# Two conv blocks on one core: images cut in halves on partition groups, 3x3 convolutions as nine taps on 32x32 array tiles

## The chip, the cores and the metric

The kernel runs on one core of a Trainium2 chip. The metric is device time in microseconds, the median of several runs. All data is fp32, apart from one small bf16 mask constant.

## The reference, cut to what matters

Input x is (8, 32, 32, 32): 8 images, 32 channels, 32 rows, 32 columns. Two blocks follow each other.

```python
# block L0
xn = ln_last(x, ln1_g, ln1_b)                  # over the 32 columns of a row
q, k, v = [conv3x3(conv1x1(xn, w1), w3) for q, k, v]   # no bias: folded into one 3x3 each
score = einsum('bhpd,bhpe->bhde', k, q) / scale # 8 heads, d = 4 neighbouring columns
attn = einsum('bhpd,bhde->bhpe', v, softmax(score))
x = conv1x1(attn, o_w) + x
xn = ln_last(x, ln2_g, ln2_b)
gate, info = gelu(conv3x3(conv1x1(xn, g1), g3)), conv3x3(conv1x1(xn, i1), i3)   # 64 channels each
x = conv1x1(gate * info, r1) + x
# block L1
out = leaky_relu(instance_norm(conv3x3(x, conv1_w) + b), 0.2)
out1 = conv3x3(out, conv2_w) + b
mask = sigmoid(conv3x3(out, mask_w) + b)
xm = out * mask
q, k, v = conv1x1(xm), conv1x1(pad(xm)), conv1x1(pad(xm))
attn = softmax over the 3x3 neighbours of sum_c q * k
return x + out1 * mask + (1 - mask) * sum over neighbours attn * v
```

## The kernel before, in words

The images are worked on in four pairs. A partition is (row block r, channel c) with four blocks of 8 rows, so every partition holds 8 rows of both images: 128 partitions by 512 values.

A 3x3 convolution multiplies on TensorE (PE) with K = 3 x 32 partitions: before it, the tensor is copied into a "planes" buffer (`sh_ln2`, `sh_x2`, `sh_in`) that holds the whole image three times, shifted by one column from one group of 32 partitions to the next. `shift_copies` (L278) does it with copies of 32 partitions by about 512 values, spread over VectorE (DVE, L283) and ScalarE (ACT, L483). The shift in y is an offset in the plane, so three matmuls of K = 96 or 128 accumulate one output. LN1's result goes to `sh_ln1` in a like way, by columns modulo 4 (`slot_copies`, L295), with four groups: two of its copies are DMAs of SyncE (SP, L333), the others are on DVE (L298) and ACT.

The matmuls: `qk` (L1160, 128x128), `v_by_head`, `conv1`, `mask_conv` and `conv2` (L1149, L1260, M = 32, four outputs on four column tiles of the array), `gate_info` (L1217, K = 96, M = 128, 512 columns), `reduce_1`. The window attention works on units of 4x8 pixels with 6x10 keys: `window_q`, `window_k`, `window_scores`, `window_v`, `probs_transposed`, `window_out`. Weights of the 1x1 and 3x3 convolutions of block L0 are multiplied together once at the start on PE and copied by `folded_qkv` and `other_constants` on DVE. An instance norm's scale is multiplied into the weights by GpSimd (POOL); POOL also takes the powers -1/2 of the norms (L392) and the residual arithmetic.

The order on every engine is written out by hand, in `step(pair)` of each engine's block: while pair n is in block L1, pair n+1 is in the second half of L0 and pair n+2 in its first half. A loop runs the first of these steps, the second is written behind it, and then the last two pairs' back halves follow in an order of their own. Engines meet by counting semaphores only; each engine waits in program order, so what stands behind a waiting instruction waits as well.

Of the kernel before, what the change touches and what calls it, by code (L numbers as in the profile page):

```python
# [68 lines left out]

def build(nc, x, shape_consts, vectors, w1_qkv, w3_qkv, w1_gi, w3_gi, conv_w, l1_qkv, r1_t, out):
    with ExitStack() as ctx:
        def sb(name, shape, dt=F32):
            return ctx.enter_context(nc.sbuf_tensor(name, shape, dt))  # L100
# [1387 lines left out]
```

## Time and profile before

| | us |
|---|---|
| median of 3 runs | 258.87 (258.56 to 259.05) |
| the profiled execution | 257.9 |
| its span, first to last instruction | 256.4 |
| DVE busy | 192.4 (75%) |
| PE busy (matmul) | 182.8 (71%) |
| ACT busy | 129.3 (50%) |
| POOL busy | 76.1 (30%) |
| mean granted TensorE clock | 0.90 of full speed |

The page gives one profiled execution. Busy times are of one engine; engines overlap. The chain of waits is followed back from the last instruction, at each step to what released it. "issue" is time in which an engine waited for nothing that the profile shows. A source matmul in fp32 appears as two MATMULs, each with its weight load (LDWEIGHTS, row PEld); matmuls on different tiles of the array overlap, so a group's busy time is less than count times mean.

### The profile page before, as it was taken

The page shows a single profiled execution, that of the slowest core. Times are in us where ns is not written, and L with a number is a line of the kernel's source. Part 1 is how long each engine was busy: PE and PEld are TensorE (multiplying, and loading weights), DVE is VectorE, ACT ScalarE, POOL GpSimd, SP SyncE. Part 2 cuts the span into 40 slices and gives each one's busy share as a digit, 9 for nine tenths or more (in the row PEclk, how much of TensorE's full clock was granted, in tenths as well). Part 3 has the DMA queues.
Part 4 walks back from the last instruction along what each step waited for, and adds up shares of the span by engine and source line. Part 5 has one row for each costly group of instructions (what it writes and reads, how often), then busy time and mean ns, then how long its engine had stood idle before and what let it go on. Part 6 is the DMA issues. An engine that isn't in the chain of part 4 may idle for free.

```text
span 256.4 us, 4585 instructions
## 1 busy us (share of the span) xinstructions
PE 182.8 (71%) x1738; PEld 111.0 (43%) x1738; DVE 192.4 (75%) x426; ACT 129.3 (50%) x256; POOL 76.1 (30%) x56
## 2 busy tenths in 40 slices
PE   0508749897568957966998589976179977297763
PEld 0308529343146536434584448442034534146632
DVE  5498694883998999996979956549999348883552
ACT  2043161641675845566745563267545467514750
POOL 4754804031008026400182231000917100302341
PEclk9999997999889999995899957999659999867995
DMA  6311021000030000000002000000010000000101
GB/s 196 75 25 36 4 61 41 0 3 0 1 102 3 1 0 3 0 23 0 3 0 84 1 1 3 0 0 3 0 41 4 0 0 4 0 0 3 45 0 43
DMA packets 5190, 5.17 MB, mean 20 GB/s; under 512 B 3184, under 2 KB 3408, under 8 KB 5168
## 3 DMA queue, kind: packets, MB, share of 16 engines
q1 hardware_dynamic: 4928, 4.29, 5.9%
q10 hardware_dynamic: 240, 0.58, 0.8%
q8 instruction: 14, 0.23, 0.4%
q14 instruction: 8, 0.07, 0.1%
HBM read 3.30 MB, written 1.05 MB: 17 GB/s over the span
## 4 chain that ended last, share of the span: by engine, by line
DVE 43%; PE 36%; ACT 8%; issue 7%; DMA 3%; POOL 1%; SPq 1%; ACTq 0%; DVEq 0%
PE ps L1224 12%; DVE sh_in L283 6%; PE ps L1171 5%; PE ps L1260 5%; DVE sh_ln L298 3%; DVE sh_ln L283 3%; DMA w3b<-in_w_gi 3%; ACT sh_x L483 2%; PE ps L1151 2%; DVE ln_out L764 2%; PE ps L1232 2%; DVE sh_x L283 2%; PE ps L1316 2%; PE ps L1300 2%; DVE gi L866 2%
## 5 line engine op out<-in xcount | busy, mean ns | idle before, releaser
L392 POOL TENSOR_TENSOR ln_s<-ln_s,neg_half 128x16 f32<-128x16 f32 x8 | 23.4, 2924 | 98.5 <-DVE ln_s L747 98.5
L1224 PE MATMUL ps<-sh_ln,w_gi 96*128 96x512 f32 x96 | 42.4, 596 | 0.5 <-DVE sm L822 0.5
L483 ACT ACTIVATE sh_ln<-ln_out 32x512 f32<-32x512 f32 (+1 forms) x44 | 27.4, 622 | 22.0 <-DVE ln_out L772 15.3
L1171 PE MATMUL ps<-w_qk,sh_ln 128*128 128x128 f32 x192 | 26.6, 302 | 12.8 <-ACT sh_ln L483 12.8
L1260 PE MATMUL ps<-sh_in,w_in 128*32 128x256 f32 x384 | 26.2, 432 | 11.4 <-DVE sh_in L283 11.4
L1171 PEld LDWEIGHTS ps<-w_qk,sh_ln 128*128 128x128 f32 x192 | 25.4, 216 | 16.4 <-issue 16.4
L1224 PEld LDWEIGHTS ps<-sh_ln,w_gi 96*128 96x128 f32 x96 | 17.9, 190 | 22.1 <-issue 21.9
L1260 PEld LDWEIGHTS ps<-sh_in,w_in 128*32 128x32 f32 x384 | 13.0, 124 | 23.3 <-DVE sh_in L283 12.5
L866 DVE TENSOR_TENSOR gi<-ps,gate 64x512 f32<-64x512 f32 x16 | 11.1, 694 | 15.0 <-ACT gate L518 14.7
L518 ACT ACTIVATE gate<-ps 64x512 f32<-64x512 f32 x16 | 9.3, 587 | 20.2 <-PE ps L1224 20.2
L283 DVE COPY sh_in<-act_c 32x496 f32<-32x496 f32 (+1 forms) x28 | 17.2, 614 | 0.5
L1151 PE MATMUL ps<-sh_x,w_conv 128*32 128x512 f32 x96 | 12.7, 664 | 5.7 <-DVE sh_x L283 4.4
L483 ACT ACTIVATE sh_x<-x 32x496 f32<-32x496 f32 (+1 forms) x20 | 12.3, 616 | 5.1 <-DVE x L873 4.9
L483 ACT ACTIVATE sh_in<-act_c 32x496 f32<-32x496 f32 (+1 forms) x20 | 12.3, 616 | 4.8 <-DVE act_c L931 4.5
L298 DVE COPY sh_ln<-ln_out 32x512 f32<-32x512 f32 x32 | 13.4, 418 | 0.5
L416 POOL TENSOR_TENSOR omm<-ones,msk 128x512 f32<-128x512 f32 x4 | 6.6, 1648 | 22.7 <-DVE msk L949 22.6
L499 ACT ACTIVATE qk_t<-ps 128x512 f32<-128x512 f32 x8 | 4.8, 596 | 15.5 <-PE ps L1171 15.5
L283 DVE COPY sh_x<-x 32x496 f32<-32x496 f32 (+1 forms) x28 | 11.5, 411 | 0.5
L283 DVE COPY sh_ln<-ln_out 32x496 f32<-32x496 f32 (+1 forms) x28 | 11.5, 411 | 0.5
L1181 PE MATMUL ps<-sh_ln,w_v 128*32 128x512 f32 x96 | 11.1, 596 | 0.0
L1316 PE MATMUL ps<-k_h,q_bd 128*64 128x60 f32 x256 | 10.8, 246 | 0.0
L398 POOL TENSOR_TENSOR inorm_v<-inorm_v,neg_half 128x2 f32<-128x2 f32 x4 | 4.3, 1076 | 21.9 <-DVE inorm_v L924 21.9
(129 smaller groups left out, 358.5 us busy)
## 6 DMA issues: line engine op xcount, KB each, us to landing
x_norm<-in_x SPq DMA_DIRECT2D x4, 256.0 KB, 2.7
x_res<-in_x SPq DMA_DIRECT2D x4, 256.0 KB, 2.5
out_x<-out_s SPq DMA_DIRECT2D x4, 256.0 KB, 2.0
sh_ln<-ln_out SPq DMA_DIRECT2D x8, 64.0 KB, 2.1
kc<-in_shape_consts ACTq DMA_DIRECT2D x1, 450.0 KB, 6.6
w3b<-in_w_gi SPq DMA_DIRECT2D x1, 288.0 KB, 6.5
vec<-in_vectors SPq DMA_DIRECT2D x1, 131.5 KB, 3.3
w3a<-in_w_qkv ACTq DMA_DIRECT2D x1, 108.0 KB, 3.2
```

The lines of the kernel that those rows point to most:

```text
L283: ins = copy(plane(planes)[C * s:C * s + C, :, 1 + RH * r:1 + RH * r + RH, cut_left:cut_left + n], src[C * r:C * r + C, :, :].rearrange("p ...
L298: ins = copy(slot_planes(s, r), slots_of(s, r))
L392: nc.gpsimd.tensor_tensor(ln_s[n][:, 3, :], ln_s[n][:, 2, :], neg_half[:, :], ALU.pow)\
L483: return nc.scalar.activation(o, i, ACT.Copy)
L518: nc.scalar.activation(gate[EC:P, n, :], ps[0:EC, GI_BANKS[n], :], ACT.Gelu).then_inc(g_gelu.sem, 1)
L866: nc.vector.tensor_tensor(gi[EC * (n % 2):EC * (n % 2) + EC, n // 2, :], ps[EC:P, GI_BANKS[n], :], gate[EC:P, n, :], ALU.mult).then_inc(g_ ...
L1151: mm = nc.tensor.matmul(ps[C * r:C * r + C, bank, :], weight(dy), plane(planes)[:, :, RH * r + dy:RH * r + dy + RH, 0:W], start=(dy == 0), ...
L1171: mm = nc.tensor.matmul(to, sh_ln1[:, d, i, WD * y:WD * y + P], w_qk[:, dy, :, :, :].rearrange("p d m c -> p (d m c)"), start=(dy == 0), s ...
L1181: mm = nc.tensor.matmul(ps[C * d:C * d + C, 2, :], w_v[:, dy, :], sh_ln1[:, d, :, WD * dy:WD * dy + WD * H], start=(dy == 0), stop=(dy == 2))
L1224: mm = nc.tensor.matmul(ps[:, GI_BANKS[2 * i + h], :], w_gi[:, dy, :, :].rearrange("p m o -> p (m o)"), xs[:, i, y:y + H // 2, 0:W], start ...
L1260: mm = nc.tensor.matmul(ps[C * r:C * r + C, bank, BLK * i:BLK * i + BLK], w_in[:, i, k, dy, :], plane(sh_in)[:, i, RH * r + dy:RH * r + dy ...
L1316: mm = nc.tensor.matmul(ps[C * r:C * r + 2 * C, 5 + bank, KEYS * n:KEYS * n + KEYS], q_bd[:, u, r:r + 2, :].rearrange("p r m -> p (r m)"), ...
```

## The change

- A partition is now (image i, half h, channel c): group g = 2i + h of 32 partitions holds 16 rows of one image. `ln2_out`, `x2` and `xm` are stored with a border of one pixel, (16 + 2) x 34; the row across the cut between the halves is copied by `edge_copies`, four copies of 32 partitions by 34 values on ACT. `x_in` holds all four pairs, and most buffers exist twice, by pair modulo 2.
- A 3x3 convolution is nine matmuls with K = 32, one for each tap, read straight from the bordered tile with offsets in y and x: `gate_info` on the four row tiles of the array (M = 128), `conv1` and the refine convolutions (mask and conv2) on all 16 tiles of 32x32, with weights repeated on the four partition groups. Their outputs are strips: four strips of 4 rows (`STRIP` = 128 values) for each group, in four banks. `conv1` turns the layout from (group, strip) to (strip, group); the refine convolutions turn it back, with an identity matmul for the activation itself.
- The planes of `sh_x2`, `sh_in` and `sh_ln2` and their copies are gone. Those of LN1 stay: for pair 0 by DVE, ACT and 4 DMAs, for the other pairs by 16 DMAs of 64 KB each from SP.
- The instance norm is applied by ACT as scale and bias when it reads conv1's result from PSUM (POOL multiplies mean and rstd for the bias); the weights are no longer scaled. `act_s` has its rows above and below copied by ACT (`rows_above`) and DVE (`rows_below`).
- `window_scores` uses 32x32 tiles, `window_out` K = 60 and M = 32 with 32 columns, `attn_out` M = 32. q is no longer spread out in a block-diagonal buffer; `key_windows` is 4 ACT instructions a pair, not 16.
- POOL's clears of the large planes shrink to borders. x is loaded by four DMAs a pair, the result stored by four.
- There is no loop; each engine's program is one list over all four pairs, in a new order. The front halves of all pairs are finished earlier, and the back halves of pairs 2 and 3 run interleaved at the end, with PSUM banks 4 to 7 for pairs 0 to 2 and 0 to 3 for pair 3.

The core of the diff (indentation cut by 12):

```diff
+HALF = HH * W
+STRIP = HALF // R
+SH = HH // R
...
-def shift_copies(copy, src, planes, s, row_blocks):
-cut_left, cut_right = max(1 - s, 0), max(s - 1, 0)
-n = W - cut_left - cut_right
-for r in row_blocks:
-    ins = copy(plane(planes)[C * s:C * s + C, :, 1 + RH * r:1 + RH * r + RH, cut_left:cut_left + n],
-               src[C * r:C * r + C, :, :].rearrange("p i (y x) -> p i y x", x=W)
-               [:, :, :, cut_right:cut_right + n])
-return ins
-def slot_copies(copy, s, row_blocks):
-for r in row_blocks:
-    ins = copy(slot_planes(s, r), slots_of(s, r))
-return ins
+def edge_copies(copy, t):
+for g in (0, 2):
+    copy(t[rows32(g), HH + 1, :], t[rows32(g + 1), 1, :])
+    ins = copy(t[rows32(g + 1), 0, :], t[rows32(g), HH, :])
+return ins
...
-        sp.dma_start(slot_planes(1, r), slots_of(1, r)).then_inc(planes_by["ln1"]["dma"].sem, 16)
+def ln1_planes(pair):
+    wait_done(sp, g_ln[0], pair)
+    wait_done(sp, g_v4, pair - 2)
+    for g in range(R):
+        for s in range(R):
+            sp.dma_start(half_planes(pair, s, g), half_slots(pair, s, g)).then_inc(s_ln1[pair], 16)
...
+load(0, (0, 1))
+sp.dma_start(vec[:, :], vectors).then_inc(s_vec, 16)
+load(1, range(R))
+sp.dma_start(w1b[:, :], w1_gi).then_inc(s_wb, 16)
+sp.dma_start(w3b[:, :, :, :], w3_gi).then_inc(s_wb, 16)
+sp.wait_ge(s_pad, 4)
+wait_done(sp, g_ln[0], 0)
+for g in range(R):
+    sp.dma_start(half_planes(0, 1, g), half_slots(0, 1, g)).then_inc(s_planes["dma"], 16)
+load(2, range(R))
+sp.wait_ge(s_zero_bd, Z_BD)
+for r in range(R):
+    sp.dma_start(w_bd[rows32(r), :, rows32(r)], l1_qkv).then_inc(s_diag, 16)
+for h in range(2):
+    sp.dma_start(w_r1[EC * h:EC * h + EC, h, :], r1_t).then_inc(s_diag, 16)
+ln1_planes(1)
+for r in range(R):
+    for dx in range(3):
+        sp.dma_start(w_conv[rows32(r), dx, :, :, :], conv_w[C * dx:C * dx + C]).then_inc(s_diag, 16)
+load(3, range(R))
+ln1_planes(2)
+ln1_planes(3)
...
+def ln2_edges(pair):
+    wait_done(act, g_ln[1], pair)
+    edge_copies(copy, ln2_out).then_inc(g_edge2.sem, 1)
+def rows_above(pair):
+    t = act_s[pair % 2]
+    wait_done(act, g_lr, pair)
+    for j in range(1, R):
+        copy(t[rows32(j), 0, :, :], t[rows32(j - 1), SH, :, :])
+    copy(t[rows32(0), 0, 1:R:2, :], t[rows32(R - 1), SH, 0:R:2, :]).then_inc(g_up.sem, 1)
...
+def other_constants():
+    dve.wait_ge(s_fold, 2)
+    for s in range(3):
+        gi_f = ps[:, 4 + s, 0:6 * EC].rearrange("p (m y o) -> p m y o", m=2, o=EC)
+        nc.vector.tensor_copy(w_gi[:, :, s, :, :].rearrange("p y m o -> p m y o"), gi_f)\
+          .then_inc(s_wready, 1)
...
+def rows_below(pair):
+    t = act_s[pair % 2]
+    wait_done(dve, g_lr, pair)
+    for j in range(R - 1):
+        nc.vector.tensor_copy(t[rows32(j), SH + 1, :, :], t[rows32(j + 1), 1, :, :])
+    nc.vector.tensor_copy(t[rows32(R - 1), SH + 1, 0:R:2, :], t[rows32(0), 1, 1:R:2, :]).then_inc(g_down.sem, 1)
...
+folded_qkv()
+ln1_center(1)
+ln_var(0, 1)
+other_constants()
+ln1_apply(1)
+dve.wait_ge(s_wready, W_ALL)
+heads(0)
+ln1_center(2)
+ln2_center(0)
+ln_var(0, 2)
+ln_var(1, 0)
+dve.wait_ge(s_zero, BORDERS + 1)
+ln1_apply(2)
+ln2_apply(0)
+heads(1)
+ln1_center(3)
+ln_var(0, 3)
+ln1_apply(3)
+gated(0)
+x2_sum(0)
...
+inorm(2)
+inorm_mean(2)
+variance(2)
+inorm(3)
+inorm_mean(3)
+variance(3)
+activation(2)
+activation(3)
+masked(2)
+masked(3)
...
+def fold_gate_info():
+    pe.wait_ge(s_wb, 32)
+    pe.wait_ge(s_zero_bd, Z_BD + 6)
+    for m in range(2):
+        for s in range(3):
+            for r in range(R):
+                mm = nc.tensor.matmul(ps[rows32(r), 4 + s, 3 * EC * m:3 * EC * m + 3 * EC],
+                                      w1b[:, C * m:C * m + C], w3b[:, s, m, :], start=True, stop=True)
+    mm.then_inc(s_fold, 1)
...
-    for h in range(2):
-        for dy in range(3):
-            y = H // 2 * h + dy
-            mm = nc.tensor.matmul(ps[:, GI_BANKS[2 * i + h], :],
-                                  w_gi[:, dy, :, :].rearrange("p m o -> p (m o)"),
-                                  xs[:, i, y:y + H // 2, 0:W], start=(dy == 0), stop=(dy == 2))
-        mm.then_inc(g_i.sem, 1)
+def gate_info(pair, dy):
+    if dy == 1:
+        wait_done(pe, g_ln[1], pair)
+    else:
+        wait_done(pe, g_edge2, pair)
+    for dx in range(3):
+        for g in range(R):
+            mm = nc.tensor.matmul(ps[:, g, :], w_gi[rows32(g), dy, dx, :, :].rearrange("p m o -> p (m o)"),
+                                  ln2_out[rows32(g), dy:dy + HH, dx:dx + W],
+                                  start=(dy == 1 and dx == 0), stop=(dy == 2 and dx == 2))
+            if dy == 2 and dx == 2:
+                mm.then_inc(g_i.sem, 1)
-    for dy in range(3):
-        for r in range(R):
-            mm = nc.tensor.matmul(ps[C * r:C * r + C, bank, :], weight(dy),
-                                  plane(planes)[:, :, RH * r + dy:RH * r + dy + RH, 0:W],
-                                  start=(dy == 0), stop=(dy == 2))
+    for dy in (1, 0, 2):
+        wait_done(pe, g_x2e, pair)
+        for dx in range(3):
+            for j in range(R):
+                for g in range(R):
+                    mm = nc.tensor.matmul(ps[rows32(j), b + g, S_CONV:S_CONV + STRIP],
+                                          w_conv[rows32(g), dx, 0, dy, :],
+                                          t[rows32(g), SH * j + dy:SH * j + dy + SH, dx:dx + W],
+                                          start=(dy == 1 and dx == 0), stop=(dy == 2 and dx == 2))
-    for i in range(2):
-        for dy in range(3):
-            for r in range(R):
-                mm = nc.tensor.matmul(ps[C * r:C * r + C, bank, BLK * i:BLK * i + BLK],
-                                      w_in[:, i, k, dy, :],
-                                      plane(sh_in)[:, i, RH * r + dy:RH * r + dy + RH, 0:W],
-                                      start=(dy == 0), stop=(dy == 2))
+    for dy in (1, 0, 2):
+        if dy == 0:
+            wait_done(pe, g_up, pair)
+        if dy == 2:
+            wait_done(pe, g_down, pair)
+        for dx in range(3):
+            for g in range(R):
+                for j in range(R):
+                    mm = nc.tensor.matmul(ps[rows32(g), b + j, col:col + STRIP],
+                                          w_conv[rows32(j), dx, k, dy, :],
+                                          t[rows32(j), dy:dy + SH, g, dx:dx + W],
+                                          start=(dy == 1 and dx == 0), stop=(dy == 2 and dx == 2))
...
+    for g in range(R):
+        for j in range(R):
+            nc.tensor.matmul(ps[rows32(g), b + j, S_ACT:S_ACT + STRIP],
+                             kc[rows32(j), K_ID + C * j:K_ID + C * j + C], t[rows32(j), 1:1 + SH, g, 1:1 + W],
+                             start=True, stop=True)
+    refine_conv(pair, 2, S_MASK)
+    refine_conv(pair, 1, S_CONV).then_inc(g_rf.sem, 1)
...
+pe.wait_ge(s_ln1[1], 256)
+for i in range(2):
+    qk_banks_read(1, i)
+    qk(1, i)
+attn_out(0)
+v_by_head(1)
+gram(1)
+by_head(1)
+pe.wait_ge(s_ln1[2], 256)
+for i in range(2):
+    qk_banks_read(2, i)
+    qk(2, i)
+pe.wait_ge(s_wready, W_ALL)
+pe.wait_ge(s_diag, 16 * (R + 2 + 3 * R))
+front_read(0, 1, 2)
+for dy in (1, 0, 2):
+    gate_info(0, dy)
+reduce_1(0)
...
```

On PE, after `reduce_1(0)`: attn_out(1), v_by_head(2), conv1(0), gram(2), average_mean(0), by_head(2), average_var(0), gate_info(1), refine(0), reduce_1(1), attn_out(2), qk(3, 0), window_q(0), window_k(0), qk(3, 1), window_scores(0), window_v(0), v_by_head(3), gram(3), by_head(3), probs_transposed(0), window_out(0), conv1(1), gate_info(2, 1), average_mean(1), gate_info(2, 0), average_var(1), gate_info(2, 2), refine(1), reduce_1(2), attn_out(3), the window steps of pair 1 with gate_info(3) between window_v(1) and probs_transposed(1), reduce_1(3), then conv1(2), its averages, conv1(3), its averages, refine(2), refine(3), q and k windows of 2 and 3, scores and v of 2, of 3, transposes and window_out of 2, of 3.

## Rows read from the trace of the kernel before

**Rows 1.** the page's busy row: us, share of the span, instructions

```profile
PE 182.8 (71%) x1738; PEld 111.0 (43%) x1738; DVE 192.4 (75%) x426; ACT 129.3 (50%) x256; POOL 76.1 (30%) x56
```

**Rows 2.** the page's chain of waits, share of the span by engine

```profile
DVE 43%; PE 36%; ACT 8%; issue 7%; DMA 3%; POOL 1%; SPq 1%; ACTq 0%; DVEq 0%
```

**Rows 3.** timeline of PE, the starts of conv1 (start us, us, what)

```profile
67.40 4.32 PE L1151 MATMUL ps<-sh_x,w_conv 128*32 128x512 f32 x24 [2.96 <-DVE sh_x L283]
...
123.62 2.78 PE L1151 MATMUL ps<-sh_x,w_conv 128*32 128x512 f32 x24 [0.34 <-DVE sh_x L283]
...
175.24 2.78 PE L1151 MATMUL ps<-sh_x,w_conv 128*32 128x512 f32 x24 [1.10 <-DVE sh_x L283]
```

**Rows 4.** windows: stretch, us, busy (instructions) by engine, clock, DMA share, GB/s

```profile
0.00:67.40 67.40, 40.00 (x246) 26.11 (x247) 48.58 (x109) 25.32 (x41) 25.02 (x18) 0.97 0.16 42
67.40:123.60 56.20, 44.35 (x424) 26.14 (x425) 51.27 (x115) 35.03 (x70) 14.07 (x9) 0.91 0.06 15
123.60:175.20 51.60, 44.41 (x424) 27.27 (x424) 37.75 (x86) 27.72 (x58) 13.71 (x10) 0.90 0.04 12
175.20:256.40 81.20, 54.02 (x644) 31.46 (x644) 54.79 (x119) 41.18 (x89) 23.30 (x19) 0.83 0.03 11
```

**Rows 5.** groups by line: count, busy us, mean ns, idle us before them

```profile
L1224 PE MATMUL ps<-sh_ln,w_gi 96*128 96x512 f32 x96 | 42.4, 596 | 0.5 <-DVE sm L822 0.5
L483 ACT ACTIVATE sh_ln<-ln_out 32x512 f32<-32x512 f32 (+1 forms) x44 | 27.4, 622 | 22.0 <-DVE ln_out L772 15.3 <-DVE ln_out L764 6.3
...
L283 DVE COPY sh_in<-act_c 32x496 f32<-32x496 f32 (+1 forms) x28 | 17.2, 614 | 0.5
L298 DVE COPY sh_ln<-ln_out 32x512 f32<-32x512 f32 x32 | 13.4, 418 | 0.5
...
L866 DVE TENSOR_TENSOR gi<-ps,gate 64x512 f32<-64x512 f32 x16 | 11.1, 694 | 15.0 <-ACT gate L518 14.7
...
L563 ACT ACTIVATE xw<-xm 128x60 f32<-128x60 f32 x64 | 9.6, 247 | 0.0
...
L518 ACT ACT_TABLE_LOAD x4 | 5.1, 1283 | 0.1
...
L513 ACT ACTIVATE sm<-sm 128x8 f32<-128x8 f32 x4 | 0.8, 208 | 4.3 <-DVE sm L824 4.3
```

**Rows 6.** chain of waits in order of time (start us, us, what)

```profile
41.13 2.91 POOL ln_s L392
...
240.43 0.67 DVE wsm L989
```

**Rows 7.** windows of window_out's matmuls alone, at two clocks

```profile
171.90:173.10 1.20, 1.10 (x64) 0.97 (x64) 1.00 0.00 0
250.00:252.00 2.00, 1.92 (x64) 1.72 (x64) 0.50 0.04 8
```

**Rows 8.** timeline of the SP queue's issues

```profile
0.73 0.39 SPq L312 DMA_DIRECT2D x_norm<-in_x  x1
...
3.53 2.57 SPq L322 DMA_DIRECT2D w_bd<-in_l_qkv  x4
...
16.47 1.35 SPq L333 DMA_DIRECT2D sh_ln<-ln_out  x2
```

**Rows 9.** DMA view: a queue's packets, MB, share; an issue's KB and landing

```profile
q8 instruction: 14, 0.23, 0.4%
...
sh_ln<-ln_out SPq DMA_DIRECT2D x8, 64.0 KB, 2.1
```

**Rows 10.** timeline of the start

```profile
4.55 0.69 DVE L734 TENSOR_REDUCE ln_s<-x_norm 128x16 f32<-128x512 f32 x1 [1.35 <-DMA vec<-in_vectors]
...
13.31 2.94 DVE L771 COPY ln_out<-ln_out 128x112 f32<-128x112 f32 x1
...
20.41 7.36 PE L1171 MATMUL ps<-w_qk,sh_ln 128*128 128x128 f32 x48 [8.33 <-ACT sh_ln L483]
...
27.82 0.50 DVE L771 COPY ln_out<-ln_out 128x112 f32<-128x112 f32 x1
```

More of the change, by code:

```diff
@@ L540, in q_evac @@
             def q_evac(pair):
-                act.wait_ge(g_q.sem, g_q.done(pair))
-                act.wait_ge(g_s.sem, g_s.before(pair))
-                for r in range(R // 2):
-                    rows = slice(C * r, C * r + C)
-                    nc.scalar.activation(q_bd[rows, :, r, :],
-                                         ps[rows, 4, :].rearrange("p (u m) -> p u m", u=UNITS), ACT.Identity,
-                                         bias=vec[rows, V_BQ:V_BQ + 1]).then_inc(g_q_sb.sem, 1)
@@ new lines, in _ @@
+            window_softmax(0)
+            ln2_apply(2)
+            v_evac(0)
+            window_probs(0)
+            heads(3)
+            inorm(1)
+            inorm_mean(1)
+            variance(1)
+            activation(1)
+            gated(2)
+            masked(1)
+            x2_sum(2)
+            ln2_center(3)
+            ln_var(1, 3)
+            window_softmax(1)
+            ln2_apply(3)
+            v_evac(1)
+            window_probs(1)
+            gated(3)
+            x2_sum(3)
@@ L1166, in qk @@
+                mm.then_inc(s_fold, 1)
+            def qk(pair, i):
+                for h in range(2):
                     for d in range(0, D, 2):
@@ new lines, in _ @@
+            by_head(3)
+            probs_transposed(0)
+            window_out(0)
+            back_banks_read(0)
+            conv1(1)
+            front_read(2, 3, 3)
+            gate_info(2, 1)
+            average_mean(1)
+            gate_info(2, 0)
+            average_var(1)
+            gate_info(2, 2)
+            refine(1)
+            reduce_1(2)
+            attn_out(3)
+            window_q(1)
+            window_k(1)
+            window_scores(1)
+            window_v(1)
+            front_read(3, 3, 3)
@@ new lines, in _ @@
+            for dy in (1, 0, 2):
+                gate_info(3, dy)
+            probs_transposed(1)
+            window_out(1)
+            reduce_1(3)
+            back_banks_read(1)
+            conv1(2)
+            average_mean(2)
+            average_var(2)
+            conv1(3)
+            average_mean(3)
+            average_var(3)
+            refine(2)
+            refine(3)
+            window_q(2)
+            window_k(2)
+            window_q(3)
+            window_k(3)
+            window_scores(2)
```

1467 lines of the change are left out of this document (633 added, 834 removed).

## The prediction

> **What bounds the kernel now.** The busy row [rows 1] has DVE at 192.4 of 256.4 us and PE at 182.8, neither full; the chain of waits [rows 2] gives DVE 43% and PE 36%. They hand work to each other in order, and the question is what that hand-over becomes. Cut at the starts of conv1 of pairs 0, 1 and 2 [rows 3], the windows [rows 4] are front A 67.4 us, stage B 56.2, stage C 51.6, tail D 81.2 (the back halves of two pairs). I price the new program in the same four pieces.
>
> **What it takes away and adds, by engine.** DVE and ACT made all shifted planes. On DVE that is 13.4 us for LN1's rows and 17.2 for act's [rows 5], with two more L283 groups of 11.5: 53.6; with the q_bd copies, centring and scaling some 65 of 192 us go. On ACT it is 27.4 and two groups of 12.3, some 50 of 129. In their place come edge copies of 32 partitions by 34 to 136 elements. No row has them on ACT; they lie between 208 ns for 8 elements and 247 for 60 (the larger ones below 627) [rows 5]; I take 0.22, and 0.30 for 136 elements. The added POOL product of two elements has no row; between nothing and the 2.9 us of the power [rows 6] I take 0.25, as it is a plain product.
>
> PE gets many more, smaller matmuls, because the shift in x moves from the plane's partitions into nine taps. A source matmul is two MATMULs in the trace (gate/info's 12 a pair: 96/4 = 24). MATMULs a pair: gate/info 24 to 72 (K 32, M 128, 512 columns), conv1 24 to 288, refine 96 to 608 (K 32, M 32, 128 columns), scores 64 to 128, window_out 64 to 128. The price hangs on how many row tiles run side by side, and the trace has only column tiles. Its rows: a full-array pass of 512 columns is 42.4/96 = 0.44 us [rows 5]; 64 MATMULs of 64 columns on four column tiles take 1.10 us at clock 1.0 and 1.92 at 0.5 [rows 7]. By the first, 64 columns on a quarter of the array stream in 0.44/8/4 = 14 ns, so the 1.10 is streaming (0.9) and one drain, and to issue a MATMUL with its weight load costs 14 ns or less. Bounds: 16 tiles side by side stream 128 columns in 0.11 us, 6.9 ns a MATMUL: conv1 2.0 us, refine 4.2, gate/info 9 x 2 x 0.44 = 7.9; no overlap of row tiles, 27.5 ns: conv1 7.9, refine 16.7, gate/info 31.7. I take 8.3 ns, near the first, because column tiles come that near to their limit: conv1 2.4, refine 5.0, gate/info 7.9 (10.6 before).
>
> [...]
>
> **Front A.** Here a wait is added. LN1's planes of pairs 1 to 3 were two DMAs and copies; now they are 16 DMAs a pair from the one SP queue. Two took 1.35 us to issue and four 2.57: 0.64 each [rows 8], and one lands 2.1 after its issue [rows 9]. So 15 x 0.64 + 2.1 = 11.7 us lie between LN1's end and qk. Behind that wait PE holds attn_out and v_by_head, for them waits LN2 of the pair before, and behind that on DVE LN1 of the next pair. The steps:
> - vec is issued behind two quarters of x, 0.75 later: LN1(0) starts at 5.3 (before 4.55 [rows 10]). Three operations of 0.7, squares 0.6, variance: 3.0; POOL's power 2.95 [rows 6]; apply 1.9; slot copies 0.6 (2.94 under POOL's clears, 0.5 without [rows 10], and the clears are gone): 13.8.
> - First planes by eight DVE copies 3.5, folded weights 0.9: qk(0) at 18.2 (before 20.4). It takes 7.4 as now [rows 10], v_by_head 2.8, the folding of the gate weights, now behind them, 1.9: 30.4. DVE waits for it in other_constants: 2.6, then apply LN1(1) 2.4: 35.4. The scores of pair 0 hide behind the next wait.
> - planes(1) 11.7: 47.1. qk(1) 7.2 (PE starts cold again), attn_out 1.1: 55.4.
> - x1 and centre 2.9, variance 0.9, power 2.95, apply LN1(2) 2.4: 64.6. planes(2) 11.7: 76.3. qk(2) 7: 83.3.
> - ACT's exp of heads(1) stands behind the evacuation of qk(2): 0.8; head_mix 2.3, then on DVE LN1(3), 2.1 + 0.9 + 2.95 + 2.4, ahead of gated(0): 94.8. gate/info(0) hides beside that. gated 4 x 0.7 [rows 5], reduce 1.1: 98.7; attn_out(1) and v_by_head(2) 3.9: conv1(0) at 102.6.
> So A costs 35 us more, 23 of them the two DMA waits.
>
> **Stages B to D**, walked the same way: an operation of 512 columns is 0.6 to 0.7 us on DVE and ACT [rows 5], a small one 0.2, a hand-over 0.05, POOL's power 3.0 (1.1 on two elements), a table load 1.3 [rows 5].
> B, from conv1(0)'s start: conv1, statistics, averages and heads(2), LN2(1) interleaved, to the variance 9.7; power and product 1.5, inorm_apply 0.9, leaky relu and rows above 2.0; only then does ACT copy LN2's edges (0.9), for which gate/info(1) waits 2.8 with dy 0 and 2: edges 15.0, gate 20.3, refine 25.3. tanh, out1, mask 2.2: 27.5. PE meanwhile runs reduce, attn_out, qk(3,0), q and k windows to 32.8, qk(3,1) 2.7, scores 2.6: 38.1. On DVE softmax, LN2(2), v_evac to 42.4, probabilities 3.1, the start of heads(3) 0.9; by_head, transposes, evacuation 2.1: 48.5; window_out 1.3, its evacuation 1.0: 50.9.
> C: conv1, two thirds of gate/info and the averages 8.3; variance to leaky relu 3.4; refine 5.1: 16.8; table, tanh, out1, mask 3.2: 20.0; q and k windows and evacuations 5.2; scores(1) 1.4, softmax 2.7, LN2(3) 1.4: 30.7; gate/info(3) 7.9: 38.6; transposes, window_out, evacuation 4.0; table and gelus, gates, reduce 5.8: 48.4.
> D: conv1 and statistics of pair 2, then of 3 (activation(2) stands behind variance(3)) 11.5; leaky relu and rows 2.0; two refines, the first in part beside the rows, to 22.6; tanh to mask of pair 3 and the q, k evacuations to 27.7; scores(2), v(2), scores(3), v(3) on PE 9.0, DVE ending softmax(3) at 38.7; v_evac and probabilities 4.3, transposes and evacuation 1.2, window_out 1.4, final 1.6, four stores 4.3: 51.5. Before, 16 us lie between the last maximum and the end [rows 6]; here 15.4.
>
> Sum: 102.6 + 50.9 + 48.4 + 51.5 = 253.4, all of B to D at full clock. Now D has clock 0.83 with PE busy 54 of 81 us [rows 4]; the new program has more gaps ahead of dense bursts (refine(2), the last transposes, reduce(3), conv1(2)), and a burst at 0.5 takes nearly twice as long [rows 7]: I add 6, between 0 and 12. 259.4; the profiled execution is 1.5 above its span (257.9 and 256.4): 260.9; the median of the runs is 1.0 above that execution: **262 us**.
>
> **Rivals.**
> (1) The front is cheaper than walked. If DMAs follow each other at 0.35 us (x_norm's issue alone took 0.39 [rows 8]) and the stages overlap a little better, A ends at 91 and B to D give 147: 238, with the 2.5 of above **240**. For it: the tail alone gives back 30 us, and DVE falls to some 125. Against: 0.64 is much the same in each burst of the trace. It decides from A below 99. 0.36.
> (2) PE is slower on small tiles. 5500 MATMULs for 1738 need some 0.7 MB of instructions against 0.23 in 14 packets, each 0.4% x 16 x 256 / 14 = 1.2 us long [rows 9]. A refine uses 4.7 packets in 5 us. If they come one per 2.5 us, a MATMUL costs 20 ns: conv1 5.6, refine 12, so 10 us in B, 10 in C, 20 in D: **300**. Half of that, 280, where row tiles overlap only in part. 0.20. Against: no MATMUL of the trace waits there, but none comes so fast.
> (3) Not a rival in sign: tiles at 7 ns and a warm PE, 253. Within the forecast's own range.
> The forecast, 250 to 274, holds 0.44. The range that leaves out a tenth at either end is 236 to 292. Less than 0.2%, 0.5 us, can't be told from no change: 0.04. Faster 0.39 (case 1 and the lower end of the forecast), slower 0.57.
>
> **What would show it.** Right: PE idle some 10 us before qk(1) and qk(2), released by a DMA; conv1(0) starting near 102; DVE busy near 125; D near 55. Wrong: planes landing less than 8 us after LN1's end; a refine above 7 us at clock 1.0; PE gaps with "issue" as releaser inside a refine.

## The result, and the profile after

| | before | after |
|---|---|---|
| median | 258.96 us (258.56 to 259.19, 4 runs) | 324.51 us (320.67 to 326.11, 4 runs) |
| profiled execution, its span | 257.9, 256.4 | 320.67, 318.9 |
| its mean granted TensorE clock, 1.00 at full speed | 0.900 | 0.853 |
| ratio | | 1.2433, 95% interval 1.2347 to 1.2519 |

The changed kernel is a quarter slower. The forecast was 262 us, and its range ended at 292. Here and below a ratio compares only the fast runs of two kernels (some executions are slower at a lower granted clock, as 326.11 us at 0.835 beside 320.67 at 0.853), so it isn't the quotient of the two medians.

First the page of the kernel after: the busy row, the instruction queue and the chain's shares; then three groups of PE (count, busy us, mean ns, idle us before them and what ended it). "PEld" is PE's weight loads.

```profile
PE 198.0 (62%) x5630; PEld 142.3 (45%) x5630; DVE 123.8 (39%) x295; ACT 82.4 (26%) x186; POOL 52.7 (17%) x60
...
q8 instruction: 44, 0.72, 1.0%
...
PE 50%; DVE 18%; issue 13%; SPq 6%; POOL 5%; ACT 4%; DMA 2%; POOLq 0%; DVEq 0%; ACTq 0%
...
L1116 PE MATMUL ps<-act_s,w_conv 32*32 32x128 f32 x2304 | 37.8, 298 | 23.0 <-issue 23.0
...
L1063 PE MATMUL ps<-ln_out,w_gi 32*128 32x512 f32 x288 | 35.9, 642 | 5.6 <-DVE ln_out L753 4.5
...
L1089 PE MATMUL ps<-x,w_conv 32*32 32x128 f32 x1152 | 20.3, 321 | 7.3 <-issue 6.3
```

DVE lost 68.6 us of its work against [rows 1], and ACT 46.9, as intended. PE has 15 us more, and the chain's "issue" share went from 7% [rows 2] to 13% of a longer span, 41 us. The two small-tile convolutions (refine L1116, conv1 L1089) have 29.3 us of idle time that ends with "issue": PE waited for nothing that a semaphore or a DMA of the kernel explains.

The windows of the kernel after, cut at the same events as [rows 4], the starts of conv1 of pairs 0, 1 and 2:

```profile
0.00:104.74 104.74, 51.86 (x426) 37.23 (x427) 45.72 (x107) 17.38 (x34) 17.18 (x31) 0.80 0.22 55
104.74:169.76 65.02, 48.26 (x1402) 34.29 (x1399) 28.84 (x75) 22.79 (x53) 10.34 (x7) 0.90 0.03 7
169.76:234.80 65.04, 45.08 (x1386) 27.89 (x1386) 23.97 (x48) 21.98 (x47) 12.79 (x10) 0.92 0.04 11
234.80:318.90 84.10, 52.79 (x2424) 42.94 (x2420) 25.32 (x66) 20.20 (x52) 12.40 (x12) 0.82 0.04 10
```

| stage | before | forecast | after | off by |
|---|---|---|---|---|
| A, front | 67.4 | 102.6 | 104.7 | 2.1 |
| B | 56.2 | 50.9 | 65.0 | 14.1 |
| C | 51.6 | 48.4 | 65.0 | 16.6 |
| D, tail | 81.2 | 51.5 | 84.1 | 32.6 |

A is as walked. The error lies in B, C and D, which hold one, one and two refine convolutions. The PE timeline of pair 0's refine in the kernel after shows what one looks like (start us, us, what, count, idle before and its end):

```profile
127.84 2.24 PE L1116 MATMUL ps<-act_s,w_conv 32*32 32x128 f32 x149
131.36 1.92 PE L1116 MATMUL ps<-act_s,w_conv 32*32 32x128 f32 x128 [1.28 <-issue]
134.81 1.92 PE L1116 MATMUL ps<-act_s,w_conv 32*32 32x128 f32 x128 [1.53 <-issue]
138.26 1.92 PE L1116 MATMUL ps<-act_s,w_conv 32*32 32x128 f32 x128 [1.53 <-issue]
141.72 0.89 PE L1116 MATMUL ps<-act_s,w_conv 32*32 32x128 f32 x42 [1.54 <-issue]
```

PE runs exactly 128 MATMULs in 1.92 us, stands still, and starts the next 128 just 3.45 us after the last start. With their weight loads these are 256 instructions. From the identity matmuls at 127.40 to the end, refine takes 15.2 us. The DMA view of 127 to 143 us of the same kernel has nothing in it but the instruction queue (the first line is GB/s in 40 slices of 0.4 us, a packet standing in the slice in which it starts):

```profile
GB/s 0 0 0 0 0 41 0 0 0 0 0 0 0 41 0 0 0 0 0 0 0 0 41 0 0 0 0 0 0 0 41 0 0 0 0 0 0 0 0 0
...
q8 instruction: 4, 0.07, 1.5%
```

Four packets of some 16 KB, at about 129.0, 132.5, 135.9 and 139.3, one to a burst and never two together: each starts about 1.1 us after a burst does, takes 1.0 us (1.5% of 16 engines over 16 us, by four), and the next burst starts some 1.4 us behind its end. That makes the step of 3.45.

### The profile page after: what moved, and what is told of

Read it like the earlier page. It is cut to its first block, busy times and chain, and to the rows that moved or that the text cites. A ratio compares the mean times of both kernels' runs of the same rounds, so it can differ in the third digit from the quotient of the medians.

```text
span 318.9 us, 12069 instructions
## 1 busy us (share of the span) xinstructions
PE 198.0 (62%) x5630; PEld 142.3 (45%) x5630; DVE 123.8 (39%) x295; ACT 82.4 (26%) x186; POOL 52.7 (17%) x60
## 3 DMA queue, kind: packets, MB, share of 16 engines
HBM read 2.59 MB, written 1.05 MB: 11 GB/s over the span
## 4 chain that ended last, share of the span: by engine, by line
PE 50%; DVE 18%; issue 13%; SPq 6%; POOL 5%; ACT 4%; DMA 2%; POOLq 0%; DVEq 0%; ACTq 0%
PE ps L1116 12%; PE ps L1004 9%; PE ps L1063 8%; PE ps L1089 6%; SPq L241 6%; POOL ln_s L286 3%; PE ps L1161 2%; DVE gi L760 2%; DVE ln_d L651 2%; PE ps L1017 2%; PE ps L1072 2%; DVE ln_out L674 1%; PE ps L1197 1%; DMA sh_ln<-ln_out 1%; PE ps L1138 1%
## 5 line engine op out<-in xcount | busy, mean ns | idle before, releaser
L1116 PE MATMUL ps<-act_s,w_conv 32*32 32x128 f32 x2304 | 37.8, 298 | 23.0 <-issue 23.0
L1116 PEld LDWEIGHTS ps<-act_s,w_conv 32*32 32x32 f32 x2304 | 30.7, 107 | 29.4 <-issue 27.3
L1004 PEld LDWEIGHTS ps<-w_qk,sh_ln 128*128 128x128 f32 x192 | 29.3, 245 | 30.1 <-DMA sh_ln<-ln_out 19.0
L1063 PE MATMUL ps<-ln_out,w_gi 32*128 32x512 f32 x288 | 35.9, 642 | 5.6 <-DVE ln_out L753 4.5
L1063 PEld LDWEIGHTS ps<-ln_out,w_gi 32*128 32x128 f32 x288 | 16.2, 199 | 21.1 <-issue 19.9
L1089 PE MATMUL ps<-x,w_conv 32*32 32x128 f32 x1152 | 20.3, 321 | 7.3 <-issue 6.3
L1089 PEld LDWEIGHTS ps<-x,w_conv 32*32 32x32 f32 x1152 | 16.1, 113 | 13.0 <-issue 11.8
L1072 PE MATMUL ps<-gi,w_r 128*32 128x512 f32 x32 | 6.0, 833 | 11.2 <-DVE gi L760 11.2
L418 ACT ACTIVATE hn<-ps,inorm_v 128x256 f32<-128x256 f32 x8 | 4.1, 566 | 24.7 <-POOL inorm_v L295 24.6
L1034 PEld LDWEIGHTS ps<-sc_d,kc 128*128 128x128 f32 x8 | 1.8, 280 | 18.4 <-DVE sc_d L701 14.1
L366 ACT ACTIVATE p_t<-ps 128x512 f32<-128x512 f32 x8 | 4.6, 596 | 20.9 <-PE ps L1182 20.9
```

Of the source, the lines that this page charges most:

```text
L366: return nc.scalar.activation(o, i, ACT.Copy)
L1004: mm = nc.tensor.matmul(to, sh_ln1[pair % 2][:, d, i, WD * y:WD * y + P], w_qk[:, dy, :, :, :].rearrange("p d m c -> p (d m c)"), start=(d ...
L1063: mm = nc.tensor.matmul(ps[:, g, :], w_gi[rows32(g), dy, dx, :, :].rearrange("p m o -> p (m o)"), ln2_out[rows32(g), dy:dy + HH, dx:dx + W ...
L1072: mm = nc.tensor.matmul(ps[rows32(g), 1, :], w_r1[:, g % 2, :], gi[:, g // 2, :], start=True, stop=True)
L1089: mm = nc.tensor.matmul(ps[rows32(j), b + g, S_CONV:S_CONV + STRIP], w_conv[rows32(g), dx, 0, dy, :], t[rows32(g), SH * j + dy:SH * j + dy ...
L1116: mm = nc.tensor.matmul(ps[rows32(g), b + j, col:col + STRIP], w_conv[rows32(j), dx, k, dy, :], t[rows32(j), dy:dy + SH, g, dx:dx + W], st ...
```

## Experiments

S names the theory that PE starves for instructions: a packet of 128 MATMULs with their weight loads every 3.45 us, whatever they are. Of the rivals, T says that the small tiles are slow of themselves, and W that something else holds PE up; their forms are spelled out in the expectations. Where a kernel ran once, its one time is given, to be held against the profiled execution of the kernel after, 320.67. That was the fastest of its four, which go up to 326.11, so a few us of a single run prove nothing. "..." in an edit marks what is left out.

**One row of taps.** The conv1 and refine loops of the changed kernel run over one row of taps, so two thirds of the taps are missing from the result.

```diff
...
-for dy in (1, 0, 2):
+for dy in (1,):
     for dx in range(3):
...
```

> The kernel after, with only the middle tap row (dy = 1) of conv1 and of the two refine convolutions; two thirds of these taps are left out of the result. MATMULs a pair: conv1 96 for 288, refine 224 for 608. Theory S (PE's instructions arrive in packets of 128 MATMULs, one per 3.45 us): a refine falls from 15.2 us to about 5.5, conv1 from 6.1 to about 2.5, and the span from 319 to 262 to 270, since nothing else changes and the chain runs through them. Theory T (the 32x32 tiles themselves are slow, 27 ns a MATMUL): the same fall, but with no issue gaps of 1.5 us after each 128 MATMULs. Theory W (my walk of the rest was wrong, and other waits hold B to D): the span stays above 285.

Measured: 263.22 us. Its windows, cut as above:

```profile
0.00:104.63 104.63, 51.54 (x426) 36.07 (x426) 46.16 (x107) 17.38 (x34) 17.18 (x31) 0.80 0.22 56
104.63:155.38 50.75, 39.25 (x826) 27.02 (x823) 28.29 (x74) 22.80 (x53) 10.34 (x7) 0.85 0.03 6
155.38:208.62 53.24, 38.82 (x810) 21.34 (x810) 24.08 (x48) 21.98 (x47) 12.79 (x10) 0.85 0.05 12
208.62:261.30 52.68, 34.55 (x1272) 27.24 (x1268) 25.07 (x66) 20.17 (x52) 12.41 (x12) 0.73 0.05 14
```

2304 MATMULs fewer give back 57.4 us, 25 ns each, three times the 8.3 ns of the forecast. A is untouched, so nearly all of what was wrong lies in these two convolutions. The instruction queue has 26 packets for 44: 18 fewer, and 2304 / 128 is 18. D falls to 52.7 though its granted clock is 0.73 for 0.82, so the half clock isn't what made D long.

**The kernel before, refine cut small.** No row tiles, no K of 32: the old column-tile matmuls, each cut from 256 columns to 64, four times as many.

```diff
-for dy in range(3):
-    for r in range(R):
+for y in range(0, RH, 2):
+    for dy in range(3):
+        for r in range(R):
...
```

> The kernel before, with each of the 96-MATMUL refine convolutions (mask and conv2 of a pair) cut into four times as many matmuls of 64 columns in place of 256: 384 MATMULs a pair, same weights, same column tiles, no row tiles, same streaming. Theory S: the two convolutions of a pair take about 10 us in place of 5.6, with gaps released by issue after each 128 MATMULs, and the time rises from 259 to 272 to 280. Theory T: column tiles are not slow (64 MATMULs in 1.10 us), so 384 take about 5.5 to 6 us and the time stays within 259 to 262.

Measured: 257.45 us, against 260.42 of the kernel before beside it, which in other runs took 253.6 to 260.4: no change that can be told. S's forecast, 272 to 280, failed. But the gaps are there, in the PE timeline of this kernel:

```profile
92.05 2.00 PE L1262 MATMUL ps<-sh_in,w_in 128*32 128x64 f32 x128 [1.28 <-issue]
95.78 0.52 PE L1262 MATMUL ps<-sh_in,w_in 128*32 128x64 f32 x18 [1.73 <-issue]
```

Again a burst of 128 MATMULs between stops of 1.3 and 1.7 us, and a step of 3.7. Packets rise from 14 [rows 9] to 23, 9 for 1152 more MATMULs. So the stops belong neither to row tiles nor to tiles of 32x32. The time didn't follow: only 5.5 us of such gaps in four pairs, since the first 150 to 285 MATMULs of a stretch come from the supply in hand and 384 a pair leave little behind them. The mechanism is shown here, not its price.

**Two queues for LN1's planes.** Half of the 16 transfers a pair issue from ACT's queue.

```diff
...
-for s in range(R):
+for s in range(2):
     sp.dma_start(half_planes(pair, s, g), half_slots(pair, s, g)).then_inc(s_ln1[pair], 16)
...
+for s in range(2, R):
+    act.dma_start(half_planes(pair, s, g), half_slots(pair, s, g)).then_inc(s_ln1[pair], 16)
...
```

> The kernel after, with the 16 DMAs of LN1's planes of a pair issued half from SP and half from ACT. If issue at 0.6 us each sets the wait before qk(1) and qk(2), both waits shrink by 8 issues, 5 us, and conv1(0) starts near 95 in place of 104.7, the time falls by 8 to 10 us to about 311 to 314. If the transfers themselves set it, nothing moves in A and the time stays at 320 to 326.

Measured: 308.19 us, below the 311 to 314 expected. The SP queue of the kernel after:

```profile
34.99 10.34 SPq L241 DMA_DIRECT2D sh_ln<-ln_out  x16
```

and both queues of this one, and its qk(1):

```profile
34.45 5.22 SPq L241 DMA_DIRECT2D sh_ln<-ln_out  x8
34.45 5.53 ACTq L507 DMA_DIRECT2D sh_ln<-ln_out  x8
...
42.16 7.55 PE L1014 MATMUL ps<-w_qk,sh_ln 128*128 128x128 f32 x48 [6.45 <-DMA sh_ln<-ln_out]
```

Issue was the price, 0.65 us a transfer on one queue, and halves on two. The waits ahead of qk(1) and qk(2) fall from 10.40 and 8.37 us to 6.45 and 3.98, and conv1(0) starts at 95.63, 9.1 us earlier. The other 3.4 us came in the stages behind: 1.6 less in B and 2.1 less in D, where the mean granted clock is 0.92 for 0.90 and 0.85 for 0.82, and 0.3 more in C; that is within what the runs of one kernel differ by.

**Column tiles in the inner loop.** Shown is conv1's loop; the refine loop is swapped the same way.

```diff
...
-for j in range(R):
-    for g in range(R):
+for g in range(R):
+    for j in range(R):
...
```

> The kernel after, with the two inner loops of conv1 and of the refine convolutions swapped: consecutive matmuls now go to different column tiles of one row tile (and one bank), not to different row tiles. Theory S (packets of 128 MATMULs, one per 3.45 us whatever their speed): within a burst the 13 ns a MATMUL may change either way, but the step from burst to burst stays 3.45 to 3.75 us and the time stays at 318 to 326. Theory T (the array's pace decides): the time moves by 10 us or more with the burst's pace.

Measured: 327.55 us, 1.5 above S's range, with a mean granted clock of 0.764 for 0.853. Pair 0's refine in this kernel:

```profile
129.60 1.92 PE L1116 MATMUL ps<-act_s,w_conv 32*32 32x128 f32 x128 [1.25 <-issue]
133.33 2.33 PE L1116 MATMUL ps<-act_s,w_conv 32*32 32x128 f32 x128 [1.81 <-issue]
136.78 2.81 PE L1116 MATMUL ps<-act_s,w_conv 32*32 32x128 f32 x128 [1.12 <-issue]
140.51 1.34 PE L1116 MATMUL ps<-act_s,w_conv 32*32 32x128 f32 x42 [0.91 <-issue]
```

The order of the tiles changes neither the burst (1.92 us, 15 ns a MATMUL and not the 13 of the expectation) nor the step. Then the granted clock fell from 1.00 to 0.50, and the bursts grew to 2.33 and 2.81 us; the steps stayed at 3.73, 3.45 and 3.73, and the stops shrank. The slower array did not lengthen them while the supply was the limit. The 6.9 us above 320.67 come with the lower clock (PE is busy 216.8 us for 198.0); whether the order had a part in that clock is open.

**Refine in bf16.** The activation and the weights of the refine stage are rounded to bf16: one MATMUL for each source matmul in place of two, 304 a pair for 608, the identity's among them.

```diff
-act_s = two("act_s", [P, SH + 2, R, PW])
+act_s = [sb(f"act_s_{n}", [P, SH + 2, R, PW], BF16) for n in range(2)]
+w_ref = sb("w_ref", [P, 3, 3, 3, C], BF16)
...
```

> [...] Theory S: a refine still needs 304 x 27 = 8.2 us with gaps after each 128 MATMULs, and the time falls by 4 x 7 = 28 us to about 292 to 297. [...]

Measured: 286.34 us. Pair 0's refine in this kernel, and the end of pair 3's, where two stand one behind the other:

```profile
126.49 1.64 PE L1120 MATMUL ps<-act_s,w_ref 32*32 32x128 bf16 x165
130.49 1.42 PE L1120 MATMUL ps<-act_s,w_ref 32*32 32x128 bf16 x123 [2.35 <-issue]
...
246.11 1.47 PE L1120 MATMUL ps<-act_s,w_ref 32*32 32x128 bf16 x128 [1.77 <-issue]
249.57 1.47 PE L1120 MATMUL ps<-act_s,w_ref 32*32 32x128 bf16 x128 [1.98 <-issue]
253.30 0.32 PE L1120 MATMUL ps<-act_s,w_ref 32*32 32x128 bf16 x9 [2.26 <-issue]
```

The burst of 128 is shorter (1.47 us at a granted clock of 0.50, for 1.92 at 1.00 in fp32), the stop longer by as much, and the steps are 3.46 and 3.73 as in fp32: the type doesn't enter the supply. Refine(0) takes 5.5 us, less than the expectation's S had for it and less than half of 15.2, because the first 165 of its 288 come from the supply in hand; a total 6 us below what S gave fits that. 34.3 us for 1216 MATMULs are 28 ns each, near the 25 of the row of taps.

**Refine's taps in a hardware loop.** The same number of MATMULs run; 5 taps of 9 are written out. The waits for the rows above and below (`g_up`, `g_down`) now stand ahead of all taps.

```diff
...
+tap(1, 0, start=True)
+with pe.Fori(0, 3):
+    tap(1, 1)
+    tap(1, 2)
+tap(2, 1)
+return tap(2, 2, stop=True)
```

> The changed kernel with the same count of MATMULs executed in each refine convolution, but their taps in a hardware loop: one tap written out, a loop of three passes over a body of two taps (64 MATMULs), two taps written out. The taps repeat, so the result of the convolution isn't the reference's. S (PE starves for its instruction packets, which bring 128 MATMULs each 3.45 us): the body is fetched once if a branch back finds it in the buffer, so 5 taps of 9 are fetched, refine falls from 15.2 us to 9 to 11 and the time to 290 to 302. W (the gaps come from running 128 small MATMULs in a row, whatever fetched them): refine stays near 15 us, time 316 to 326. S with a branch that throws the buffered instructions away: gaps of 2 us or more at each of the six branches back, refine 17 us or more, time above 322.

Measured: 300.30 us. Pair 0's refine in this kernel, and the end of pair 3's; then its windows:

```profile
127.76 8.83 PE L1114 MATMUL ps<-act_s,w_conv 32*32 32x128 f32 x575
...
263.91 3.46 PE L1114 MATMUL ps<-act_s,w_conv 32*32 32x128 f32 x214 [1.78 <-issue]
```

```profile
0.00:105.47 105.47, 51.69 (x427) 36.21 (x427) 46.17 (x107) 17.38 (x34) 17.19 (x31) 0.81 0.23 56
105.47:163.46 57.99, 46.91 (x1403) 33.25 (x1400) 28.40 (x74) 22.80 (x53) 10.35 (x7) 0.93 0.02 6
163.46:224.65 61.19, 48.17 (x1386) 29.80 (x1386) 23.48 (x48) 21.98 (x47) 12.54 (x10) 0.86 0.04 11
224.65:298.50 73.85, 51.79 (x2424) 41.06 (x2420) 25.37 (x66) 20.18 (x52) 12.45 (x12) 0.85 0.04 11
```

This settles it. In pair 0 the same tiles, columns, banks and count run through without a stop, 14.8 us becoming 8.8, and over the four pairs one stop of 1.8 us is left where there were 23.0 us of them; the kernel is 20.4 us faster, while PE's busy time over the whole of it is the same (198.6 for 198.0 us). The packets fall to 36: 8 fewer, and the 4 taps that a loop repeats are 128 MATMULs of each of 8 convolutions, 1024 / 128 = 8. The branches of the loops cost nothing that the timeline shows. It also gives the array's own price: 15.4 ns a MATMUL. W and the variant in which a branch throws the buffered instructions away are out, and so is T: its 27 ns a MATMUL lies at the prediction's bound for row tiles that don't overlap at all (27.5), but that is chance, since the same tiles take 15.4 once they are fed. The repeated taps give a wrong convolution; a loop over the nine real taps, with offsets from registers, was not tried.

**Both edits at once**, two queues and the loop.

> The changed kernel with both edits at once: LN1's plane transfers half from ScalarE's queue, and the taps of the refine convolutions in a loop over a body of two taps (taps repeat, the result isn't the reference's). If the transfers' issue and the supply of instructions are two separate costs, their gains add: 320.7 less 12.5 less 20.4 (each from the profiled execution with one edit alone), 286 to 290. If they share a cause (the instruction packets wait behind the 64 KB transfers, or the other way round), the sum falls short: 294 or more.

Measured: 291.59 us, between the two expectations. The window up to conv1(0) in this kernel, and on the PE timeline the conv1 starts behind it:

```profile
0.00:96.34 96.34, 51.62 (x427) 36.13 (x427) 46.16 (x107) 17.38 (x34) 17.19 (x31) 0.82 0.25 63
```

```profile
154.52 4.22 PE L1099 MATMUL ps<-x,w_conv 32*32 32x128 f32 x173 [0.97 <-ACT pv L497]
...
215.88 3.31 PE L1099 MATMUL ps<-x,w_conv 32*32 32x128 f32 x185
```

A is 9.1 us below that of the loop alone, the same 9.1 as with two queues alone; B, C and D are 58.2, 61.4 and 73.9 us, where the loop alone has 58.0, 61.2 and 73.9. Stage by stage the two costs add. What doesn't repeat is the 3.4 us behind the front that the expectation had counted to the two queues.

**The tap gate alone, in the kernel before.** Only the gate and info convolution reads a bordered LN2 tile on row tiles; LN2's planes go. One thing more was changed, which the expectation doesn't say: in the tail, ACT's q and k evacuations and `key_windows` of pair 2 stand ahead of pair 3's gelus, and DVE's q evacuation ahead of its gate products. That order was not run by itself.

```diff
-w_gi = sb("w_gi", [3 * C, 3, 2, EC])
+w_gi = sb("w_gi", [P, 3, 3, 2, EC])
-ln2_out = sb("ln2_out", [P, 2, BLK])
+ln2_out = sb("ln2_out", [P, 2, RH + 2, PW])
...
-planes("ln2", ln2_out, sh_ln2, g_ln[1], g_i, pair)
+for r in range(R - 1):
+    act_copy(ln2_out[C * r + C:C * r + 2 * C, :, 0, :], ln2_out[C * r:C * r + C, :, RH, :])
+    ins = act_copy(ln2_out[C * r:C * r + C, :, RH + 1, :], ln2_out[C * r + C:C * r + 2 * C, :, 1, :])
...
```

> The kernel before with one part of the change alone: gate/info as nine taps on the four row tiles, read from a bordered LN2 tile in the old layout (8 rows of both images a partition), halo rows by 6 ACT copies; no planes of LN2, all else as before. MATMULs a pair 72 for 24, 512 columns each, 8 us in all, which is far above 27 ns each. Theory S: no issue gaps in this stage, it takes 8.0 us for 10.6, and with 12 plane copies a pair gone the time falls by 6 to 14 us, to 245 to 253. Theory T (row tiles are slow of themselves): gate/info above 10.6 us and the time not below 259.

Measured: 256.14 us (4 runs) against 258.89, ratio 0.9886 [0.9789, 0.9982]. No issue gap in the gate convolution: 288 MATMULs of 512 columns are few and long, and the instruction queue has 15 packets, one more than before. But I had expected 6 to 14 us and got 3. The ACT and PE timelines of this kernel show where the gain of the loop's pass went:

```profile
111.86 1.07 ACT L517 ACTIVATE gate<-ps 64x512 f32<-64x512 f32 x2 [5.54 <-PE ps L1238]
112.95 3.82 ACT L482 ACTIVATE sh_ln<-ln_out 32x512 f32<-32x512 f32 x6
116.68 1.05 ACT L517 ACTIVATE gate<-ps 64x512 f32<-64x512 f32 x2
...
118.75 1.93 PE L1247 MATMUL ps<-gi,w_r 128*32 128x512 f32 x8 [5.88 <-DVE gi L876]
```

The four banks now finish together, at the end of the ninth tap, so the gelus can't start while the convolution runs, and two of them stand behind LN1's slot copies, as they did before.

**Gelus ahead of ACT's slot copies.**

```diff
-if norm:
-    ln1_planes(pair + 3)
 gelu(pair + 1, 2)
 gelu(pair + 1, 3)
+if norm:
+    ln1_planes(pair + 3)
```

> The kernel before with its gate and info convolution alone on row tiles of the bordered tile, and in the one pass of ScalarE's loop the LN1 slot copies (3.82 us) put behind the last two gate gelus and not ahead of them. S and W (both theories of the refine convolutions) say the same here, since no small MATMULs were added: no issue gaps, and reduce_1 of that pass follows the gate convolution by about 3.5 us and not 7, so 250 to 255 us, 3 below the same kernel without the exchange (256.1). Against it: the slot copies are then 2 us later, and if q and k of the next pair wait for them, nothing is gained.

Measured: 255.61 us (12 runs), ratio to the kernel before 0.9955 [0.9887, 1.0023], above the expected range and not told from no change, and reduce_1 waits longer, 6.68 us for 5.88. The DVE timeline of this kernel names what was next:

```profile
113.37 3.44 DVE L297 COPY sh_ln<-ln_out 32x512 f32<-32x512 f32 x8
...
116.84 2.87 DVE L876 TENSOR_TENSOR gi<-ps,gate 64x512 f32<-64x512 f32 x4
```

All gelus are done at 114.11, and the products wait for DVE's own slot copies.

**Gate products ahead of DVE's slot copies too.**

```diff
-ln1_apply(pair + 3)
+ln_apply(0, ln1_out, "ln1", pair + 3)
+ln1_neighbours(pair + 3)
 gated(pair + 1, 0)
...
 gated(pair + 1, 3)
+if norm:
+    planes("ln1", ln1_out, sh_ln1, g_ln[0], g_v4, pair + 3)
```

> The kernel before with the tap gate and with the four gelus ahead of ScalarE's slot copies, and now the four gate products ahead of VectorE's slot copies of LN1 too (once in the kernel, in the loop's one pass). In the version without the last step the gelus ended at 114.11 and the products began at 116.84, behind 3.44 us of copies. If those copies are what is late, the products end near 116.4, reduce_1 comes 2.5 to 3 us earlier, and the time is 251 to 254. If the copies, now 3 us later, are what the next pair's q and k wait for (they start at 128.4), nothing is gained: 255 to 256.

Measured: 254.47 us (251.31 to 256.39, 12 runs) against 257.79 (253.99 to 259.68, 17 runs) of the kernel before on the same chip, ratio 0.9916 [0.9862, 0.9970]. The wait ahead of reduce_1 in this kernel, and the one behind it:

```profile
112.53 1.20 PE L1250 MATMUL ps<-gi,w_r 128*32 128x512 f32 x8 [2.54 <-DVE gi L876]
117.48 1.93 PE L1358 MATMUL ps<-p_t,v_t 128*32 128x64 f32 x64 [3.75 <-ACT p_t L579]
```

The first fell from 6.68 to 2.54 us, but window_out's matmuls now wait 3.75 us for ACT's copies of p_t, which stand behind ACT's slot copies. From the gate convolution's start to conv1's, the pass takes 20.4 us here, 21.7 in the version before and 20.9 with the tap gate alone. This version has the lowest median of the study, 0.8% below the kernel before by its ratio, and it keeps that kernel's loop and its other matmuls. What is shown is that the tap gate, with its order in the tail, makes the kernel before about 1% faster; the tap gate's own ratio is 0.9886, so nothing shows that the two exchanges on top of it add anything.

## Why the prediction was wrong

**Right.** The reading of the front. From PE's timeline of the kernel after:

```profile
46.86 7.51 PE L1004 MATMUL ps<-w_qk,sh_ln 128*128 128x128 f32 x48 [10.40 <-DMA sh_ln<-ln_out]
...
76.22 8.16 PE L1004 MATMUL ps<-w_qk,sh_ln 128*128 128x128 f32 x48 [8.37 <-DMA sh_ln<-ln_out]
85.22 8.01 PE L1063 MATMUL ps<-ln_out,w_gi 32*128 32x512 f32 x72 [0.84 <-issue]
...
104.74 2.59 PE L1089 MATMUL ps<-x,w_conv 32*32 32x128 f32 x174
109.11 1.78 PE L1089 MATMUL ps<-x,w_conv 32*32 32x128 f32 x114 [1.78 <-issue]
```

A takes 104.7 us for 102.6; qk(0), qk(1), qk(2) start at 17.34, 46.86 and 76.22 for 18.2, 47.1 and 76.3, the latter two behind idle times of 10.40 and 8.37 us that a DMA ends, and the 0.64 us an issue of [rows 8] held over sixteen in a row (0.65). Two queues show that this is issue. gate/info takes 8.01 us at a granted clock of 1.00 for 7.9, so four row tiles do overlap fully at 512 columns. DVE's busy time is 123.8 for about 125. Of "PE starts cold again" the traces show a slow start: the 48 MATMULs of qk(1) take 7.51 us for 7.2, and of them 19 fill the first 4.0 us, at a mean granted clock of 0.50; in qk(0) 18 fill the first 4.0 us, at 1.00. DVE's copy of `ln_out`, 2.94 us in [rows 10] beside POOL's clears, takes 0.22 in the kernel after, at 12.50 us, with no large clear beside it; the 0.50 of [rows 10] still had one. The front costs 37 us more than before, and that alone eats the 30 us that the tail was to give back.

**The step that failed** is the price of a small MATMUL, "I take 8.3 ns". conv1 took 6.15 us for 2.4 and refine 15.2 for 5.0. Two things were mis-sized in it:

- What the array does, when nothing starves it: 15.4 ns at a granted clock of 1.00, from the looped refine, not 8.3. I took the bound by streaming (6.9) as nearly reached because 64 MATMULs on four column tiles came near theirs [rows 7]. But by that row a MATMUL with its weight load needed no more than 14 ns, and that was an upper bound for issue that I read as a cost already hidden; the 15.4 lies just above it. In bf16 it is 9.9 (165 in 1.64 us at the same clock), so the 14 is no floor either. At a granted clock of 0.50 the bursts of 128 take 22.0 ns a MATMUL in fp32 (2.81 us) and 11.5 in bf16 (1.47 us). What sets 15.4 and 9.9 is not settled; the order of tiles isn't it (128 took 1.92 us in either order). The "one drain" in the 1.10 us was an estimate of mine, what is left beside 0.9 of streaming; no run shows it by itself.
- The supply: 3.45 us for 128 MATMULs, 27 ns each, once the packets in hand are used up. Rival 2 had this mechanism, and the sign that would show it, but with a packet per 2.5 us and so 20 ns a MATMUL, refine 12 and 300 us in all. The row behind it gave only a packet's transfer, 1.2 us [rows 9]; what lies ahead of a transfer and behind it (1.1 and 1.4 us) had no row, since in the kernel before no stretch ran dry. "No MATMUL of the trace waits there" was not quite so (two of L1289 wait 0.87 us each, ended by issue), and it was no evidence against the rival: at 1738 MATMULs, few of them in a row, a starved stretch couldn't have shown.

The sum: the two groups are busy 58.1 us where 3456 MATMULs at 8.3 ns are 28.7, which is 29.4 more, some of it at the half clock (0.53 in the mean over the 4.0 us from 234.80, conv1(2)'s first 193 MATMULs, where 174 of conv1(0) took 2.59 at 1.00); their issue gaps are 29.3; A adds 2.1. That is 60.8, from which the 6 us that the forecast held for the clock come off; the profiled execution is 59.8 above its forecast of 260.9. About 5 us of the excess carry no name of their own. That gaps ahead of dense bursts lower the clock was my estimate, and no run shows the 6 us by themselves. The mean granted clocks were 0.90, 0.92 and 0.82 in B, C and D, where the sum had full clock; qk(0), behind 10.20 us of idle time, ran at 1.00, and qk(1), behind 10.40, was granted 0.50 over its first 3 us.

**Sixteen tiles.** A 128-column MATMUL by itself is an estimated 0.44 / 4 = 0.11 us by [rows 5], so 15.4 ns is a speedup of 7.1 by overlap. Four row tiles reach the full 4 that I took, at 512 columns: gate/info's 8.01 us are an estimated 7.9 by the same 0.44 (9 x 2 passes). Sixteen at 128 columns stay well below 16, and I had priced them at 8.3 ns, a speedup of 13.

**The rivals.** Rival 1, the cheaper front, is refuted: A is 104.7 us and not below 99. Rival 3 falls with the price. Of rival 2, "280 where row tiles overlap only in part" was the wrong way to halve it: both halves of the cost came, the slower array and the starved one.

## What to carry to other kernels

Before a convolution is cut into small taps, count its instructions, not only its columns: a stretch of more than some 150 to 280 MATMULs with own weight loads, written out, went at 27 to 29 ns each here, in fp32 and bf16 alike, and a full-array pass of 512 columns, 0.44 us, is 64 MATMULs of 32x32 tiles and 128 columns. Where they must be small, try to repeat a body of 64 MATMULs in a hardware loop (shown here only with the same taps repeated), and look for "issue" gaps behind bursts of exactly 128. Take such a change apart: of this one the gate convolution, with few long MATMULs, was worth keeping, at about 1%. A wait that goes in one place can come back in the next: with the gate products moved ahead of DVE's slot copies one wait fell by 4.1 us and another of 3.75 appeared.
